# A metaformer kernel on one core: the lead-in's order, the start of attentions two and three, and three norm tiles of image three

## The reference

```python
x = x + conv_attention(ln_c(x))          # layer 0
t = tokens(x); t = t + moe_ffn(ln_t(t)); x = image(t)
x = x + conv_sum(ln_c(x))                # layer 1: 7x7 + 5x3 + 3x5 + separable 7 and 5
t = tokens(x); t = t + moe_ffn(ln_t(t)); x = image(t)

# conv_attention, 12 heads of 32 in all, 96 channels:
value = dwconv3x3(x, w_v); query = dwconv3x3(x, w_q)
key = dwconv3x3(x, w_k, stride 2); off = dwconv3x3(x, w_off1, stride 2)
o = gelu(layernorm over channels(off)); pos = tanh(w_off2 @ o + ref)
v_sampled = bilinear samples of value at pos          # 28 x 28 points
out = (query @ key.T * 32 ** -0.5) @ v_sampled; y = w_out @ out

# moe_ffn: 4 experts, the best 2 kept, 96 -> 384 -> 96
out = sum over e of gate[e] * (gelu(x @ w1[e] + b1[e]) @ w2[e] + b2[e])
```

## Time and profile before

| | us |
|---|---|
| median of 3 runs | 1609.75 |
| lowest, highest | 1603.1, 1610.59 |
| profiled execution, its own time | 1609.45 |
| its span, first to last instruction | 1607.6 |
| its mean granted TensorE clock | 0.955 |

### The profile page before, as it was taken

How to read it: one execution, slowest core, us unless ns; L and a number is a source line. 1 busy time by engine, 2 the same in 40 slices (tenths; PEclk the granted TensorE clock), 3 DMA queues, 4 the chain that set the end, 5 groups by cost and what they waited for, 6 DMA issues and landing times.

```text
span 1607.6 us, 21544 instructions
## 1 busy us (share of the span) xinstructions
PE 1430.1 (89%) x6736; PEld 1059.2 (66%) x6736; DVE 1140.9 (71%) x2881; ACT 726.1 (45%) x1508; POOL 510.7 (32%) x533
## 2 busy tenths in 40 slices
PE   4977677998779999998888999999999999998998
PEld 3654654556545677665555577787888788877786
DVE  6837867489984644359896444587787877689787
ACT  5622253246533444454644244454444544356554
POOL 4051143011360000011163000254344634465575
PEclk9997777999889999999989999999999999999999
DMA  4433034134333312341351422343224422221121
GB/s 121 99 91 109 25 107 123 47 104 118 82 86 92 92 50 57 103 119 56 100 128 52 132 66 61 76 111 109 62 80 113 108 67 60 72 79 60 53 69 56
DMA packets 168547, 136.37 MB, mean 85 GB/s; under 512 B 114928, under 2 KB 162162, under 8 KB 168050
## 3 DMA queue, kind: packets, MB, share of 16 engines
q1 hardware_dynamic: 163458, 129.74, 29.6%
q0 software_dynamic: 3072, 4.82, 1.2%
q10 hardware_dynamic: 1904, 0.43, 0.1%
HBM read 95.30 MB, written 39.13 MB: 84 GB/s over the span
## 4 chain that ended last, share of the span: by engine, by line
PE 50%; issue 13%; DVE 10%; POOL 7%; ACT 5%; DMA 1%; SPq 1%; ACTq 0%; POOLq 0%; DVEq 0%
PE at_ps L1349 10%; PE y_ps L1201 7%; PE h_ps L1208 5%; PE h_ps L1210 5%; PE h_ps L1209 5%; POOL pix_mem L1075 4%; PE y_ps L1190 4%; PE y_ps L1191 3%; PE y_ps L1192 3%; PE at_ps L1268 3%; DVE vq_mem L1554 2%; ACT ln_cen L868 2%; POOL ln_rstd L1048 2%; PE lb_ps L1163 2%; PE lg_ps L1176 1%
## 5 line engine op out<-in xcount | busy, mean ns | idle before, releaser
L1003 ACT ACTIVATE hidden<-h_ps,b 128x448 f32<-128x448 f32 x609 | 384.0, 633 | 618.7 <-PE h_ps L1210 606.1
L1208 PE MATMUL h_ps<-xh,w1h 96*128 96x448 f32 x672 | 366.6, 546 | 2.6 <-ACT hidden L1003 1.3
L1048 POOL TENSOR_TENSOR ln_rstd<-ln_ve,minus_half 112x4 f32<-112x4 f32 x112 | 152.5, 1361 | 659.7 <-DVE ln_ve L1493 659.5
L1201 PE MATMUL y_ps<-hidden,w 128*96 128x448 f32 x672 | 324.1, 567 | 14.3 <-ACT hidden L1003 13.7
L1510 DVE SCALAR_TENSOR_TENSOR part<-y_ps,b,gate_t 96x448 f32<-96x448 f32 x224 | 151.5, 676 | 214.3 <-PE y_ps L1201 170.1
L1067 POOL CAST in_w<-hidden 128x448 fp32r<-128x448 f32 x273 | 200.0, 736 | 242.6 <-ACT hidden L1003 161.8
L1209 PE MATMUL h_ps<-xl,w1h 96*128 96x448 f32 x672 | 249.9, 372 | 0.0
L1210 PE MATMUL h_ps<-xh,w1l 96*128 96x448 f32 x672 | 249.4, 371 | 0.0
L1208 PEld LDWEIGHTS h_ps<-xh,w1h 96*128 96x128 f32 x672 | 130.1, 194 | 90.1 <-issue 61.2
L1209 PEld LDWEIGHTS h_ps<-xl,w1h 96*128 96x128 f32 x672 | 131.5, 196 | 66.9 <-issue 61.4
L868 ACT ACTIVATE ln_cen<-ln_cen,ln_rstd 112x96 f32<-112x96 f32 x448 | 130.3, 363 | 79.0 <-POOL ln_rstd L1048 78.8
(11 more groups left out here) (186 smaller groups left out, 2153.2 us busy)
## 6 DMA issues: line engine op xcount, KB each, us to landing
gate_t<-gates_dram SPq DMA_DIRECT2D x112, 336.0 KB, 3.2
value_pairs<-pix_mem SPq DMA_DIRECT2D x56, 168.0 KB, 3.1
x_mem<-norm_c SPq DMA_DIRECT2D x16, 420.0 KB, 4.4
res_mem<-in_x SPq DMA_DIRECT2D x4, 1176.0 KB, 11.0
x_attn<-res_mem SPq DMA_DIRECT2D x16, 294.0 KB, 2.7
res<-x_attn SPq DMA_DIRECT2D x28, 168.0 KB, 2.8
x_ffn<-ffn_out SPq DMA_DIRECT2D x28, 168.0 KB, 2.0
ln_x<-x_ffn SPq DMA_DIRECT2D x28, 168.0 KB, 2.9
```

The lines of the kernel that those rows point to most:

```text
L1003: act.activation(to[:, :], h_ps[c % H_BANKS][:, 0:TILE], ACT.Gelu, bias=b1[l][:, c:c + 1]).then_inc(gelu_done, 1)
L1048: pool.tensor_tensor(ln_rstd[n % 2][:, :], ln_ve[n % 2][:, :], minus_half[0:SUB, 0:NSUB], ALU.pow)\
L1201: pe.matmul(y_ps[e % Y_BANKS][0:C, 0:TILE], w2[l][:, c, :], hidden[c % HID_RING][:, :], start=(j == 0), stop=(j == CPE - 1)).then_inc(hid_ ...
L1208: pe.matmul(ps, hi, xh[:, ring(k)], start=True, stop=False)
```

## The change

It has four parts.

1. The lead-in's order. `expand_w_out` and its counterpart on TensorE come after step (-1,4) instead of (-1,3). Tile 4 of the norm of image 1 goes to place 1 of (-1,7). Of image 0, one of three query convolutions goes behind the turns of the values, the key convolutions one chunk later, the key diagonals from step (-1,6) to the end of (-1,5), gelu and tanh two chunks and one chunk sooner, `fold_taps` two steps sooner. Of image 1, all query taps are in stages 4 and 5. The first half of the first gates is read at the end of (-1,13).
2. `ATTN_START` replaces `ATTN_SLOT`: stage 0 of image 2 is in (0,2) and of image 3 in (2,2), stage 6 in (1,1) and (3,1). A step can have two attention stages: (0,2) has stage 6 of image 1 and stage 0 of image 2.
3. In such a step the four loads of rows are issued ahead of the stores of the output. VectorE's wait for the conv's stores, which image 3's taps need, stands directly ahead of the first tap.
4. Norm jobs. Image 2's tiles 5 and 6 come a step sooner, image 3's tiles 0 to 2 go to (0,1) and (0,2) and its others three tiles sooner, to (1,6) to (2,1), the c tiles of image 1 to (2,1) to (3,1); (3,2) has none.

```diff
@@ -66,15 +66,18 @@
-ATTN_SLOT = {2: 0, 3: 2}
+ATTN_START = {2: (0, 2), 3: (2, 2)}
...
-              (-1, 7): [("a1", 4)], (-1, 8): [("a1", 5), ("a1", 6)], (-1, 9): [("a2", 0), ("a2", 1)],
+              (-1, 7): [None, ("a1", 4)], (-1, 8): [("a1", 5), ("a1", 6)], (-1, 9): [("a2", 0), ("a2", 1)],
...
-              (-1, 13): [("f0", 3), ("f0", 4)], (-1, 14): [("f0", 5), ("f0", 6)], (0, 0): [("a2", 4)], (0, 1): [("a2", 5)],
-              (0, 2): [None, ("a2", 6)]}
+              (-1, 13): [("f0", 3), ("f0", 4)], (-1, 14): [("f0", 5), ("f0", 6)], (0, 0): [("a2", 4), ("a2", 5)],
+              (0, 1): [("a2", 6), ("a3", 0)], (0, 2): [("a3", 1), ("a3", 2)],
+              (1, 6): [("f2", 6), ("a3", 3)], (2, 0): [("a3", 4), ("a3", 5)], (2, 1): [("c1", 0), ("a3", 6)],
+              (2, 2): [("c1", 1), ("c1", 2)], (2, 6): [("f3", 6), ("c1", 3)], (3, 0): [("c1", 4), ("c1", 5)],
+              (3, 1): [("c1", 6)], (3, 2): []}
@@ -109,9 +112,9 @@
-DIRECT = (0, 2, 3)
+DIRECT = (0, 3)
...
-GATE_STEP = {(-1, LEAD - 1): (0, 0), (0, 0): (0, 1),
+GATE_STEP = {(-1, LEAD - 2): (0, 0), (0, 0): (0, 1),
@@ -129,13 +132,14 @@
-        return [(1, p + 4)]
-    for b, first in ATTN_SLOT.items():
-        if slot == first and p >= 3:
-            return [(b, p - 3)]
-        if slot == first + 1 and p < 3:
-            return [(b, p + 4)]
-    return []
+        stages = [(1, p + 4)]
+    else:
+        stages = []
+    for b, (first, step) in ATTN_START.items():
+        stage = (slot - first) * TILES + p - step
+        if 0 <= stage < TILES:
+            stages.append((b, stage))
+    return stages
@@ -452,18 +456,18 @@
-        Q_ROUNDS = {4: (0, 5), 5: (5, 8), 6: (8, 9)}
+        Q_ROUNDS = ({4: (0, 5), 5: (5, 8), 6: (8, 9)}, {4: (0, 5), 5: (5, 9)})
...
-        QUERY_CONV = {(0, 9): (0, 0), (0, 10): (0, 1), (1, 3): (0, 2), (3, 2): (1, 0), (3, 8): (1, 1), (4, 2): (1, 2)}
-        QUERY_TAKE = {(0, 11): (0, 0), (1, 2): (0, 1), (1, 5): (0, 2), (3, 8): (1, 0), (3, 11): (1, 1), (4, 5): (1, 2)}
-        KEY_CONV = {(0, 2, 10): 0, (0, 2, 11): 1, (0, 3, 0): 2, (1, 1, 4): 0, (1, 1, 5): 1, (1, 1, 7): 2}
-        KEY_TAKE = {(0, 2, 10): 0, (0, 2, 11): 1, (0, 3, 3): 2, (1, 1, 5): 0, (1, 1, 6): 1, (1, 1, 8): 2}
-        DIAG_AT = {(4, 11): ("query", 0), (5, 1): ("query", 1), (5, 4): ("query", 2), (6, 0): ("key", 0),
-                   (6, 3): ("key", 1), (6, 6): ("key", 2)}
+        QUERY_CONV = {(0, 9): (0, 0), (0, 10): (0, 1), (2, 10): (0, 2), (3, 3): (1, 0), (3, 8): (1, 1), (4, 2): (1, 2)}
+        QUERY_TAKE = {(0, 11): (0, 0), (1, 2): (0, 1), (2, 11): (0, 2), (3, 8): (1, 0), (3, 11): (1, 1), (4, 5): (1, 2)}
+        KEY_CONV = {(0, 2, 11): 0, (0, 3, 0): 1, (0, 3, 1): 2, (1, 1, 4): 0, (1, 1, 5): 1, (1, 1, 7): 2}
+        KEY_TAKE = {(0, 3, 0): 0, (0, 3, 1): 1, (0, 3, 3): 2, (1, 1, 5): 0, (1, 1, 6): 1, (1, 1, 8): 2}
+        DIAG_AT = {(4, 11): ("query", 0), (5, 1): ("query", 1), (5, 4): ("query", 2), (5, 8): ("key", 0),
+                   (5, 9): ("key", 1), (5, 10): ("key", 2)}
@@ -750,6 +754,9 @@
+                if 0 in stages and 6 in stages:
+                    for q in range(Q):
+                        load_quarter(stages[0], q)
@@ -757,7 +764,7 @@
-                if 0 in stages and slot >= 0:
+                if 0 in stages and 6 not in stages and slot >= 0:
@@ -962,11 +969,11 @@
-                    if stage == 2 and c == (10 if b == 0 else 9):
+                    if stage == 2 and c == (8 if b == 0 else 9):
...
-                    if stage == 2 and c == 11:
+                    if stage == 2 and c == (10 if b == 0 else 11):
@@ -1011,7 +1018,7 @@
-                        if slot < 0 and c == (APPLY_DEEP[job.place] if deep(job) else LEAD_APPLY[job.place] if p not in (7, 11) else 10 if p == 7 else 7) or slot >= 0 and c == APPLY and job.place == 0:
+                        if slot < 0 and c == (APPLY_DEEP[job.place] if deep(job) else LEAD_APPLY[job.place] if p not in (7, 11) else 11 if p == 7 else 7) or slot >= 0 and c == APPLY and job.place == 0:
@@ -1019,7 +1026,7 @@
-                    if (slot, p) in GATE_STEP and c == (8, 11 if u in SPLIT_SLOTS else 10)[GATE_STEP[slot, p][1]]:
+                    if (slot, p) in GATE_STEP and c == (8 if slot >= 0 else 11, 11 if u in SPLIT_SLOTS else 10)[GATE_STEP[slot, p][1]]:
@@ -1398,7 +1405,7 @@
-                if (slot, p) == (-1, 3):
+                if (slot, p) == (-1, 4):
@@ -1558,7 +1565,7 @@
-                q0, q1 = Q_ROUNDS.get(stage, (0, 0))
+                q0, q1 = Q_ROUNDS[b == 1].get(stage, (0, 0))
@@ -1787,7 +1794,7 @@
-            TAPS_LEAD = {0: dict(none, combine2=1, end=1)}
+            TAPS_LEAD = {0: dict(none, combine2=1, end=1), 1: dict(none, combine0=5, combine1=3, combine2=4, end=3)}
@@ -1811,11 +1818,10 @@
-                ops = [op for b, stage in stages for op in attn_taps(b, stage)]
+                taps = {stage: attn_taps(b, stage) for b, stage in stages}
+                ops = [op for some in taps.values() for op in some]
...
-                if by_stage.get(0) == 3:
-                    dve.wait_ge(conv_st[0], 16 * CG * PARTS)
@@ -1825,7 +1831,7 @@
-                    if ops and stage in (TAPS_SLOT if slot >= 0 else TAPS_LEAD):
+                    if taps[stage] and stage in (TAPS_SLOT if slot >= 0 else TAPS_LEAD):
@@ -1837,6 +1843,8 @@
+                        if by_stage[0] == 3:
+                            dve.wait_ge(conv_st[0], 16 * CG * PARTS)
@@ -1874,9 +1882,14 @@
-                    if owner[name] in GATE_STEP or slot < 0 and (slot, p) in GATE_STEP:
-                        gates = GATE_STEP[(slot, p) if slot < 0 else owner[name]]
-                        if name == (("normalize1", "scores")[gates[1]] if slot >= 0 else "combine1"):
+                    if (slot, p, name) == (-1, LEAD - 2, "end"):
+                        read_scores(0, 0)
+                    if (slot, p, name) == (-1, LEAD - 1, "combine0"):
+                        rank_gates(0, 0)
+                        pick_gates(0, 0)
+                    if owner[name] in GATE_STEP:
+                        gates = GATE_STEP[owner[name]]
+                        if name == ("normalize1", "scores")[gates[1]]:
@@ -1902,9 +1915,9 @@
-                if (slot, p) == (-1, 3):
+                if (slot, p) == (-1, 4):
...
-                if (slot, p) == (-1, 10):
+                if (slot, p) == (-1, 8):
```

## The result

The changed kernel took 1618.29 us (median of 7 runs, 1615.7 to 1621.46) against 1608.99 for the kernel before (7 runs, 1603.1 to 1615.91). The ratio is 1.0055 with a 95% interval of 1.0035 to 1.0074. The forecast was 1601, in a range of 1589 to 1610. The profiled execution took 1617.17 us, 7.7 above that of before.

A forecast was written before the change was run, and what follows sets the result against it. Each stage was taken as a chain of waits between engines, with VectorE filling stages 1 to 5. The terms -12 + 5.5 + 5.7 - 3.5 - 4.2 = -8.5 took 1609.45 to 1600.95, taken as 1601 us, range 1589 to 1610.

The forecast's parts named there:

- What bounds the kernel: Whole kernel: steps hand over between engines, so each stage must be asked what it waits for; busy shares say little.
- L: Lead-in, up to about 214 us: 12 us saved, 8.5 by sooner gathers less half the fold, 3.5 by gates.
- A: Steps (0,0) and (0,1): +5.5 us, 2.6 for one more norm job each and 2.9 for three query taps.
- The sign named for A: Image one's keys start no more than 7 us sooner than before, against TensorE's idling at 275.95.
- B: Step (0,2): +5.7 us, image two's taps ahead of image one's output additions making TensorE wait, 1.9 and 3.8.
- foremost sign of being wrong: Step (0,2) growing by more than 8 us would show the prediction wrong above all.
- C: (0,3) to (1,2): -3.5 us, stages 1 to 5 starting a step sooner and staying VectorE's; bounds 0 and -7.
- D: (2,2) to (3,2): -4.2 us, all of it from three norm jobs that left this stretch for slot 0.
- the second of the two foremost signs: Steps of stages 1 to 5 changing length would show the prediction wrong, as it argued they only move.
- lost cover: Loads of rows on SyncE's queue, costed at nothing; without cover, VectorE's wait at 331.07, 2.5 us an image.
- Nothing for (1,3): Step (1,3), just behind the stretch from (0,3) to (1,2): no change was forecast, 0 us.
- Rival 4: Beside images one and two's gathers, taps and norm operations block more, 3.9 us each; five give 1620.5; chance 0.12.

The follow-up runs named there:

- lead-in alone: The changed kernel with everything behind the lead-in put back (attention starts, norm tiles, rows, query taps): 1601.55 us, ratio 0.9938.
- third experiment: The changed kernel with attention three back at (2,3), its norm tiles kept in their new steps: 1612.36 us, ratio 1.0012.
- both repairs: The changed kernel with the conv's tap loads at the end of (1,0) and attention three starting at (2,3): 1605.19 us, ratio 0.9973.
- norm-tile kernel: The changed kernel with attentions two and three and image one's query taps as before, lead-in and norm tiles as changed: 1596.82 us, ratio 0.9921.
- First taps behind the additions: The changed kernel with all of image two's first taps in (0,2) behind image one's output additions: 1616.06 us, ratio 1.0042.

## Why the prediction was wrong, by its own steps

- **What bounds the kernel.** Right as far as it went: the stages are chains of waits, and a step that VectorE fills stays VectorE's. But SyncE was read as a supplier of data, not as a queue in program order.
- **L, -12.** The trace gives -12.5, and in the other kernels with this lead-in 9.4 to 11.6; the median of the lead-in alone -8.5. First and last gather came at 79.19 and 108.55, where 81 and 109 were forecast. Of its parts the expansion was under-priced (4.5 us in the trace, 2.0 in the medians, against 2), the fold is consistent with its price (0.2 to 3.3 against 2.6), and the 3.5 of the gates is given back by (0,0) in the lead-in alone. That the whole came out at 12.5 in this execution is partly luck.
- **A, +5.5.** +0.5. The three query taps cost about what they were priced at (2.3 to 2.8 us against 2.9). The two norm tiles were priced at +2.6 by rows of steps where VectorE and TensorE are both short of time; here they gave 2.5 us back by the keys (-1.4 at the keys with a start 1.1 us later), because they changed which of VectorE's taps hold GpSimd up. The sign named for A failed with it: the keys came 12.0 us sooner, not at most 7.
- **B, +5.7.** Right in mechanism, the first wait nearly to the tenth (1.70 us for 1.9; the sum's own rule, twice 0.6 off 3.2, gives 2.0). At the second it took 4.37 for 3.8 and missed the clock: 1.7 us for one product at the lower level. +6.9. The step itself grew by 10.9 us, over the 8 that the prediction had named as its foremost sign of being wrong; the 4.0 beyond B stand ahead of the keys and belong to A, whose two steps before it were shorter by 3.5.
- **C, -3.5.** -2.8. Right: stages that VectorE bounds only move. Stages 1 to 5 took 130.4 us for 130.8, stage 6 50.2 for 49.2.
- **D, -4.2.** +3.2, the second of the steps that failed. The norm tiles gave 3.0 us (third experiment), but the earlier start, which was to move the stages and no more, cost 5.9. Stages 1 to 5 took 136.8 us where 133.4 were forecast (1.0 above the 132.4 that the rows of before give, without a reason), so the second of the two foremost signs showed too; stage 6 took 50.6 for 47.5, and (3,2) 16.9 for 16.0. The trace shows one reason, which no run takes apart from the others: the loads were costed at nothing, but image three's rows stand behind the last norm tile and the conv's stores in the very step that needs them, so its taps fall into the next step. The price named for lost cover was 2.5 us.
- **Nothing for (1,3): the step that failed most.** Moving stage 6 from (1,2) to (1,1) moved its stores ahead of `load_taps`, which stands at the end of (1,1) in both kernels and is no part of the diff. The prediction looked at the queue only where loads were moved, in (0,2), and there said that behind the stores only rows for later norms wait. It measured 8.6 us alone.

In sum, by medians: lead-in -8.5, norm tiles -4.7, query taps +2.8, attention three's start +5.9; what is left to the +8.2 between 1618.29 and the 1610.1 of the experiments' own runs of before is +12.7 for attention two's start. Of it 8.6 are the tap loads that its stores now hold up, and 4.1 its own, which is also what the trace of the changed kernel shows (6.9 - 2.8). Another way round gives more: the kernel with both repairs stands 8.4 us above the norm-tile kernel; less the query taps (2.8), and with the 2.3 us that sooner tap loads gave that kernel too, if they are more than scatter, its own share is 7.9. So 4 to 8, where the prediction had 2.2 (5.7 - 3.5); this stays open.

Rival 4 had the side right on which the time ended, by luck: its mechanism is real and carries the 2.8 us of the query taps, but not the rest. Four gathers took over 4 us, where before had three. Two of them are far longer than any before, one in each moved attention (7.69 us at 404.81). The one in attention three:

```profile
807.04 7.68 POOL L1082 DMA_INDIRECT pix_mem<-value_pairs,o_idx  x1 [0.23 <-issue]
```

The keys of image three nevertheless came only 1.6 us later against its first tap (at 854.61, 148.6 us after it; before 147.0, 863.84 - 716.87).

## What to carry to other kernels

Before moving a step in a program written out by hand, list on every queue what stands fixed at the place it moves to, also what the diff doesn't touch: a DMA that waits for a round trip through DRAM was harmless behind a step without output stores and cost 8.6 and 15.0 of its 16 us behind one with them. An early start is worth nothing if the stage is bound by an engine that is already full, and less than nothing if its input or another stage's output has to share the step. Take the parts that pay apart from those that don't: the lead-in and the norm tiles alone ran in 1596.8 us, and in 1594.6 with the tap loads a step sooner. And before explaining a step by its clock or its length, look at the same step in kernels that leave it alone: (1,3) without a late load took from 25.9 to 28.9 us.

## What the runs showed of the hardware that was not expected

- A wait of TensorE can be paid twice, but the second payment is irregular. After one of 4.37 us a product of six matmuls took 3.91 us instead of 2.21, at a grant of 0.64 and 0.60; after one of 1.70 it took 2.21. In (1,3) TensorE idled 7.2 us of 36.6, 5.0 more than before, and at a granted clock of 0.81 was busy 5.6 us more. In two other kernels with the same late loads (**Attention three back**, **First taps behind the additions**) it idled 8.3 and 8.2 us there, and at 0.90 was busy only 2.0 and 2.2 more.
- GpSimd is held in whole taps: one tap more in VectorE's row of them made a gather and a norm operation 0.94 us longer each. The longest holds were two gathers of 7.68 and 7.69 us, where 4.90 had been seen; each ran beside two rows of three taps with one `part` operation (L1517) between them.
- A step with more work was shorter: with two norm tiles instead of one (0,0) took 25.0 us instead of 28.6, as the taps then stand in shorter rows and the norm tile's power on GpSimd is done sooner.
